# Another order of 68 units in a pipelined stack of convolutions, with VectorE's share of the evictions chosen unit by unit

## The reference, cut to what matters

```python
x = x + _L0_conv_ref(_gn(x), ...)   # windowed attention: qkv, scores + bias, softmax, weigh, projection
x = x + _L1_conv_ref(_gn(x), ...)   # one 3x3 convolution ("conv1")
x = x + _L2_conv_ref(_gn(x), ...)   # a grid of 4 columns x 4 rows of 3x3 convolution cells with relu
x = x + _L3_conv_ref(_gn(x), ...)   # a quantised 3x3 convolution, scaled by the maximum over all images
```

```python
for col in range(NUM_COLS):
    for row in range(NUM_ROWS):
        ...
        ins = [outs[row][0], outs[row + 1][1], outs[row - 1][-1]]   # inner rows; fewer at the edges
        outs[row] = _cell(W[col, row], b[col, row], ins)            # conv 3x3, bias, relu, split
return outs[-1][0]
```

## Time and profile before

| | |
|---|---|
| median of 3 runs | 3118.27 us (3115.51 to 3122.56) |
| profiled execution | 3120.86 us, span 3119.1 us |
| TensorE busy | 2786.1 us (89%) |
| VectorE busy | 2299.9 us (74%) |
| ScalarE busy | 2011.4 us (64%) |
| mean granted TensorE clock | 0.964 |

### The profile page before, as it was taken

One profiled execution on the slowest core, in us unless ns is written; L12 is line 12 of the kernel. 1 busy time (PEld: TensorE's weight loads), 2 busy tenths in 40 slices (PEclk: granted clock), 3 DMA queues, 4 the chain that ended last, 5 costly groups with the idle time before them and its releaser, 6 DMA issues.

```text
span 3119.1 us, 84833 instructions
## 1 busy us (share of the span) xinstructions
PE 2786.1 (89%) x39155; PEld 1185.7 (38%) x39155; DVE 2299.9 (74%) x2105; ACT 2011.4 (64%) x2318; POOL 23.5 (1%) x68
## 2 busy tenths in 40 slices
PE   4755899989998899989998999989998989889976
PEld 3742333333333333333433343333333333333333
DVE  8969985899688986889598987899599961240135
ACT  1107976766767676766776776767776775766524
POOL 0000000000000000000000000000000000000000
PEclk9877999999999999999999999999999999999998
DMA  1014656586667667675657766685657664775566
GB/s 63 11 21 63 84 79 91 72 111 89 85 84 95 94 84 99 80 105 79 84 84 92 102 89 90 86 113 74 94 74 99 90 88 64 94 107 73 79 89 181
DMA packets 37555, 268.00 MB, mean 86 GB/s; under 512 B 19280, under 2 KB 19920, under 8 KB 24784
## 3 DMA queue, kind: packets, MB, share of 16 engines
q1 hardware_dynamic: 37008, 261.77, 59.6%
q10 hardware_dynamic: 192, 0.80, 0.2%
HBM read 22.54 MB, written 12.04 MB: 11 GB/s over the span
## 4 chain that ended last, share of the span: by engine, by line
PE 70%; DVE 15%; ACT 10%; issue 3%; SPq 1%; DMA 1%; POOL 0%; ACTq 0%; POOLq 0%; DVEq 0%
PE conv_banks L856 43%; PE conv_banks L870 20%; ACT pair L706 5%; ACT half L706 4%; DVE pair L1058 2%; DVE half L1058 2%; PE side_banks L817 2%; PE stat_bank L827 1%; PE side_banks L783 1%; ACT scores L692 1%; PE conv_banks L954 1%; DMA half<-half 1%; DVE scores L1073 1%; DVE score_max L1081 1%; DVE scores L1071 1%
## 5 line engine op out<-in xcount | busy, mean ns | idle before, releaser
L706 ACT ACTIVATE pair<-conv_banks,b_cells 32x784 f32<-32x784 f32 x1316 | 1213.0, 922 | 586.9 <-PE conv_banks L870 520.0
L856 PE MATMUL conv_banks<-pair,w_cells 128*32 128x392 f32 x17664 | 1538.1, 497 | 25.2 <-issue 11.6
L870 PE MATMUL conv_banks<-half,w_cells 64*32 64x392 f32 x18432 | 880.2, 508 | 143.8 <-ACT pair L706 60.7
L856 PEld LDWEIGHTS conv_banks<-pair,w_cells 128*32 128x32 f32 x17664 | 559.6, 109 | 948.0 <-issue 904.3
L706 ACT ACTIVATE half<-conv_banks,b_cells 32x392 f32<-32x392 f32 (+1 forms) x780 | 520.4, 667 | 172.7 <-PE conv_banks L870 133.9
L870 PEld LDWEIGHTS conv_banks<-half,w_cells 64*32 64x32 f32 x18432 | 337.4, 107 | 666.6 <-issue 620.8
L1058 DVE TENSOR_SCALAR half<-conv_banks,b_cells 32x392 f32<-32x392 f32 (+1 forms) x180 | 114.4, 636 | 326.5 <-PE conv_banks L870 168.4
L1058 DVE TENSOR_SCALAR pair<-conv_banks,b_cells 32x784 f32<-32x784 f32 x220 | 227.5, 1034 | 109.3 <-PE conv_banks L870 99.1
L1071 DVE TENSOR_TENSOR scores<-qkv 128x1792 f32<-128x1792 f32 x98 | 197.8, 2019 | 71.8 <-ACT qkv L687 71.5
L692 ACT ACTIVATE scores<-scores 128x1792 f32<-128x1792 f32 x104 | 176.7, 1699 | 78.5 <-DVE scores L1155 46.1
L1097 DVE TENSOR_TENSOR scores<-scores,qkv 128x1792 f32<-128x1792 f32 x98 | 198.4, 2025 | 3.4
(11 more groups left out here) (107 smaller groups left out, 1042.3 us busy)
## 6 DMA issues: line engine op xcount, KB each, us to landing
pair<-pair SPq DMA_DIRECT2D x384, 391.9 KB, 8.6
half<-half SPq DMA_DIRECT2D x348, 192.4 KB, 5.6
x_block<-in_xa SPq DMA_DIRECT2D x8, 784.0 KB, 11.0
stream<-in_xs SPq DMA_DIRECT2D x8, 784.0 KB, 10.5
x_scratch<-stream SPq DMA_DIRECT2D x7, 784.0 KB, 6.9
pair<-x_scratch SPq DMA_DIRECT2D x7, 784.0 KB, 14.2
out_dram<-pair SPq DMA_DIRECT2D x4, 1120.0 KB, 5.3
half<-half SPq DMA_DIRECT2D x174, 7.1 KB, 4.7
```

The lines of the kernel that those rows point to most:

```text
L706: done = nc.scalar.activation(dst, src, ACT.Relu, bias=b_ap)
L856: done = nc.tensor.matmul(conv_ps[32 * q:32 * q + 32, n + b, 0:QN], w, P[row][:, QG * s + BG * (q // 2):QG * s + BG * (q // 2 + 1), BX * ( ...
L870: done = nc.tensor.matmul(conv_ps[32 * q:32 * q + 32, n + h, 0:QN], w_all[rows, at:at + 32], T[rows, QG * u + BG * (q // 2):QG * u + BG * ...
```

## The change

Three lists are replaced, and the code that reads them made finer.

- The order. Before, all units of a cell stood together. Now units of different cells alternate: column-0 units stand between units of other cells, and the two units of an output can stand apart. An asterisk marks the late units.
- VectorE's share. It is now a list of units, with the place in VectorE's own order: behind weigh 4, scores 6 and weigh 6, 17 units in a middle body (20 before). In body 6 it has 43 units (20 before), in body 7 10 (16 before), in body -1 one (none before). `move_stream` goes from behind weigh 9 to behind weigh 13.
- The side steps stand at other units, among them SyncE's "conv1", from 63 to 55 in the middle bodies.

```diff
-BODY = [((3, 0), 1), ((2, 2), 1), ((3, 1), 1), ((2, 3), 1), ((0, 0), 0), ((3, 2), 1), ((0, 1), 0), ((3, 3), 1),
-        ((0, 2), 0), ((1, 0), 0), ((0, 3), 0), ((1, 1), 0), ((1, 2), 0), ((2, 0), 0), ((1, 3), 0), ((2, 1), 0)]
+ORDER = """
+30D0* 30D1* 22D0* 22D1* 22U0* 22U1* 00R0 22R0* 22R1* 23U0* 23U1* 31D0* 31D1* 23R0* 00D0 23R1* 00D1
+32D0* 32D1* 00R1 01U0 01U1 01D0 01D1 33R0* 33R1* 01R0 10D0 10D1 02U0 01R1 02U1 02R0 10R0 02R1 02D0
+10R1 02D1 11D0 11D1 11U0 11U1 03U0 03U1 03R0 11R0 11R1 12U0 03R1 12U1 20D0 12D0 20D1 12D1 12R0 20R0
+12R1 13U0 13U1 20R1 13R0 13R1 21U0 21D0 21U1 21D1 21R0 21R1
+"""
...
-PE_MID = {2: [("qkv", 1, 0)], 7: [("proj", 0, 0), ("qkv", 2, 0)], 12: [("proj", 1, 0), ("qkv", 3, 0)],
-          27: [("proj", 2, 0), ("qkv", 4, 0)], 44: [("proj", 3, 0), ("qkv", 5, 0)],
-          49: [("proj", 4, 0), ("qkv", 6, 0)], 54: [("proj", 5, 0)], 59: [("proj", 6, 0)], 60: [("mean1", 0, 0)],
-          61: [("var1", 0, 0), ("mean0", 0, 1)], 62: [("var0", 0, 1)], 64: [("qkv", 0, 1)],
-          65: [("conv1", 0, 1)], 66: [("conv1", 1, 1)], 67: [("mean2", 0, 1), ("var2", 0, 1)]}
+PE_MID = {2: [("qkv", 1, 0)], 6: [("proj", 0, 0), ("qkv", 2, 0)], 13: [("proj", 1, 0)], 14: [("qkv", 3, 0)],
+          26: [("proj", 2, 0)], 29: [("qkv", 4, 0)], 42: [("proj", 3, 0)], 44: [("qkv", 5, 0)],
+          48: [("proj", 4, 0)], 49: [("qkv", 6, 0)], 57: [("proj", 5, 0)], 58: [("proj", 6, 0)],
+          59: [("mean1", 0, 0)], 60: [("var1", 0, 0), ("mean0", 0, 1)], 61: [("var0", 0, 1)],
+          63: [("qkv", 0, 1)], 64: [("conv1", 0, 1)], 65: [("conv1", 1, 1)], 66: [("mean2", 0, 1)],
+          67: [("var2", 0, 1)]}
...
-ACT_MID = {2: [("qkv", 1, 0), ("exp", 1, 0)], 5: [("exp", 2, 0)], 7: [("qkv", 2, 0), ("exp", 3, 0)],
-           9: [("exp", 4, 0)], 12: [("qkv", 3, 0), ("exp", 5, 0)], 19: [("exp", 6, 0)], 26: [("qkv", 4, 0)],
-           27: [("exp", 7, 0)], 38: [("exp", 8, 0)], 44: [("qkv", 5, 0), ("exp", 9, 0)], 47: [("exp", 10, 0)],
-           49: [("qkv", 6, 0), ("exp", 11, 0)], 51: [("exp", 12, 0)], 54: [("exp", 13, 0)], 64: [("qkv", 0, 1)],
-           65: [("exp", 0, 1)]}
+ACT_MID = {1: [("qkv", 1, 0)], 3: [("exp", 1, 0)], 5: [("exp", 2, 0)], 7: [("qkv", 2, 0)], 8: [("exp", 3, 0)],
+           10: [("exp", 4, 0)], 15: [("qkv", 3, 0)], 17: [("exp", 5, 0)], 24: [("exp", 6, 0)],
+           38: [("qkv", 4, 0)], 39: [("exp", 7, 0)], 41: [("exp", 8, 0)], 44: [("qkv", 5, 0), ("exp", 9, 0)],
+           46: [("exp", 10, 0)], 48: [("qkv", 6, 0)], 50: [("exp", 11, 0)], 54: [("exp", 12, 0)],
+           55: [("exp", 13, 0)], 63: [("qkv", 0, 1)], 64: [("exp", 0, 1)]}
...
-SP_MID = {35: [("x3", -1)], 48: [("xa", 2)], 63: [("conv1", 1)], 66: [("xb", 2)], 67: [("input", 1)]}
-SP_BEFORE = {35: [("x3", -1)], 62: [("conv1", 1)], 67: [("input", 1)]}
+SP_MID = {40: [("x3", -1)], 51: [("xa", 2)], 55: [("conv1", 1)], 67: [("xb", 2), ("input", 1)]}
+SP_BEFORE = {40: [("x3", -1)], 55: [("conv1", 1)], 67: [("input", 1)]}
...
+VEC_FIRST = {("s", 2): "00D0"}
+VEC_MID = {("w", 4): "23R0 00D0 23R1",
+           ("s", 6): "32D0 32D1 00R1 01U0 01U1 01D0",
+           ("w", 6): "02U0 01R1 02U1 02R0 10R0 02R1 02D0 10R1"}
+FINISH_AT = ("w", 6)
+MOVE_AT_FIRST, MOVE_AT = ("s", 13), ("w", 13)
+VEC_LATE = """30D0 22U0 22U1 23U1 31D0 31D1 23R0 00D0 23R1 32D0 32D1 00R1 01U0 01U1 01D0 01D1 10D0 10D1 02U0 01R1
+02U1 02R0 10R0 02R1 02D0 10R1 02D1 11D0 11D1 11U0 11U1 03U0 03U1 12U0 12D1 12R0 20R0 13U1 13R0 13R1
+21U0 21D1"""
+VEC_LAST = """22D0 22U1 22R0 22R1 23U1 31D1 23R0 23R1 32D0 32D1"""
...
-                for dst, src, b_ap in unit_operands(k, cell, o, u, range(2 if cell in shared_in(m) else NQ)):
+                for dst, src, b_ap in unit_operands(k, cell, o, u, range(2 if (cell, o, u) in shared_in(m) else NQ)):
...
+            def other_work(m, at):
+
+                early = isinstance(m, int) and m < 0
+                empty(m, units((VEC_FIRST if early else VEC_MID).get(at, "")))
+                if at == FINISH_AT and not early:
+                    finish(m, m)
+                if at == (MOVE_AT_FIRST if early else MOVE_AT):
+                    move_stream(m + 1)
```

More of the change, by code:

```diff
@@ L105, in strips_of, with unit, units, starts @@
     return (u, u + 2) if has_single(col, row) else (2 * u, 2 * u + 1)
-BODY = [((3, 0), 1), ((2, 2), 1), ((3, 1), 1), ((2, 3), 1), ((0, 0), 0), ((3, 2), 1), ((0, 1), 0), ((3, 3), 1),
-        ((0, 2), 0), ((1, 0), 0), ((0, 3), 0), ((1, 1), 0), ((1, 2), 0), ((2, 0), 0), ((1, 3), 0), ((2, 1), 0)]
[L111 to L119, removed]
+ORDER = """
[4 more added lines that the diff above has]
+"""
+def unit(text):
+    return (int(text[0]), int(text[1])), "RUD".index(text[2]), int(text[3])
+def units(text):
+    return [unit(t) for t in text.split()]
+UNITS = units(ORDER)
+UNITS_F = [unit(t) for t in ORDER.split() if t[4:] != "*"]
+UNITS_L = [unit(t) for t in ORDER.split() if t[4:] == "*"]
 NF, NB, NL = len(UNITS_F), len(UNITS), len(UNITS_L)
 NS = NF + (B - 1) * NB + NL
-def body_of(m):
-    return (EARLY_BODY if m < 0 else LATE_BODY if m == B - 1 else BODY) if isinstance(m, int) else BODY
 def units_in(m):
-    return units_of(body_of(m))
+    return (UNITS_F if m < 0 else UNITS_L if m == B - 1 else UNITS) if isinstance(m, int) else UNITS
+def starts(m, k):
+    done = units_in(m)
+    return done[k][0] not in [cell for cell, _, _ in done[:k]]
 def unit_base(m):
@@ L153, in count_halos @@
             wrote(m, "input", INPUT)
-        for (cell, late) in body_of(m):
-            need[m, cell] = [(key, n[key]) for key in in_places(*cell)]
-            for o in cell_outs(*cell) if cell != LAST else []:
+        for k, (cell, o, u) in enumerate(units_in(m)):
+            if starts(m, k):
+                need[m, cell] = [(key, n[key]) for key in in_places(*cell)]
+            if u == 1 and cell != LAST:
                 wrote(m, (cell, o), out_place(*cell, o))
-        if m == -1:
-            n_first = dict(n)
     return need
@@ L226, in n_shared @@
 def n_shared(m, end):
-    return sum(cell in shared_in(m) for cell, _, _ in units_in(m)[:end])
+    return sum(done in shared_in(m) for done in units_in(m)[:end])
 def vec_value(m, k):
-    ahead, per = n_shared(-1, NF), sum(cell in SHARED_MID for cell, _, _ in UNITS)
+    ahead, per = n_shared(-1, NF), len(SHARED_MID)
     if not isinstance(m, int):
@@ L880, in body @@
                         side_step(m + d, kind, j)
-                    if cell == (0, 0) and cell != seen:
+                    if cell == (0, 0) and starts(m, k):
                         wait_halos(pe, m, "input")
-                    conv_unit(m, k, cell, o, u, cell != seen).then_inc(conv_done, 1)
-                    seen = cell
+                    conv_unit(m, k, cell, o, u, starts(m, k)).then_inc(conv_done, 1)
             def first_sums(kind, k, done_sem):
@@ L1049, in normalise_stream, with empty @@
                     done.then_inc(c_ready, 1)
[L1051 to L1055, removed]
+            def empty(m, mine):
+                for cell, o, u in mine:
+                    k = units_in(m).index((cell, o, u))
                     dve.wait_ge(conv_done, unit_base(m) + k + 1)
@@ L1287, in move_stream, with late_body @@
                 done.then_inc(moved, 1)
-            def body(m):
[L1290 to L1301, removed]
+            def other_work(m, at):
[5 more added lines that the diff above has]
+                    move_stream(m + 1)
+            def late_body(m):
+                mine, end = shared_in(m), units_in(m).index((LAST, RIGHT, 1))
+                before = [u for u in mine if m == B - 1 or units_in(m).index(u) < end]
+                if m < B - 1:
+                    add_conv1(m + 1)
+                empty(m, before)
+                finish(m, m)
+                empty(m, mine[len(before):])
+                if m < B - 1:
+                    move_stream(m + 1)
+            def body(m):
                 i = m + 2
```

77 lines of the change are left out of this document (35 added, 42 removed).

## The result

The changed kernel takes 3133.11 us (median of 7 runs, 3125.78 to 3141.60); the kernel before takes 3118.27 (7 runs beside it, 3112.79 to 3122.56). The ratio is 1.0049, with a 95% interval of 1.0035 to 1.0064: 0.5% slower. The forecast was 3031 us in a range of 3002 to 3077, with a chance of 0.92 for faster. The profiled execution took 3125.78 us, with a span of 3124.0. Every median in this document is over executions that agree within 0.6%; one execution of experiment 1 took 9098 us and is in none of them.

What follows compares the result with a forecast made beforehand. TensorE was taken as the bound, with some 18 us idle per like body. Gains of 43 (five like bodies), 18, 13, 8 and 5 sum to 87 us: 3120.9 to 3033.9, or 3031 as median; range 3002 to 3077.

Steps and rivals of the forecast that it cites:

- a ring of waits between VectorE and ScalarE: Rival: late VectorE holds TensorE, then ScalarE's evictions and copies, so VectorE gets later; about 3129 us, chance 0.05.
- The half on the evictions: Like bodies: TensorE's waits for ScalarE's (27.5 us) and VectorE's (22.4 us) evictions over four bodies can be won by order.
- the last line of the walk: Like bodies: TensorE's waits under "issue" are removed by no order and stay at 1.6 us a body.
- so this costs nothing: SyncE's conv1 step from unit 63 to 55: four sends held behind it are first read 40 us later, so no cost.
- The eviction waits and the 4.26 us at 02U0: 02U0 to 11D0: 1.9 us of waits, none above 0.6; the 4.26 us wait and its slow clock go.
- The walk of a like body: 68 units walked in the new order: 12.0 us idle, body 336 us, 8.6 less than 344.6.
- the waits at the meeting points and the turns: TensorE's waits in four groups of units of a like body: about 1.0, 3.6, 1.9 and 2.7 us.
- VectorE at the last projection: Last projection, at 267 us of a like body: VectorE's wait falls from 8.18 us to at most 2.
- No copy or exponential was to come late: ScalarE's 34 copies and exponentials each end before VectorE asks; closest is chunk 5's copy, 196.1 against 197; no cost.
- Body 7: m = 7: 32D0's 6.22 us halo wait goes, the 11.66 us wait before 33R0 stays; 8 us less.
- Body -1: m = -1 (283.8 us): interleaving of cell (0, 3) and conv1 gives about 9 back, 00D0's wait costs 4; 5 us less.
- Bodies 5 and 6: m = 5 from 354.9 to 337 us, 18 less, with earlier halos; m = 6 from 323.7 to 310, 13 less.

Runs made afterwards that it cites:

- experiment 1: Changed kernel with SyncE's conv1 step back at its old places (before unit 63 in the middle bodies): 3111.7 us, ratio 0.998 to the kernel before.
- Experiment 2: Kernel before with only SyncE's conv1 step moved early, from before unit 63 to before unit 56: 3160.9 us, ratio 1.0126 to the kernel before.
- Experiment 5: Changed kernel with SyncE's conv1 step before unit 61 (43 in body -1): 3078.7 us, ratio 0.9862 to the kernel before.
- experiment 3: Changed kernel with each pair send from body 1 on moving half of its rows, same order, waits and DMAs: 3009.5 us, ratio 0.964 to the kernel before.

## Why the prediction was wrong

The direction was wrong, and so was the mechanism that decides it: none of the rivals named TensorE's own instructions. The rival that ended slower was a ring of waits between VectorE and ScalarE; TensorE's waits for their evictions fell instead of growing. The half on the evictions was right, and its gain is there: from span to span, waits for blocks cost 78.2 - 11.8 = 66.4 us more and busy time 14.6 more (2786.1 to 2800.7), and the span grew by 4.9, so all the rest gained 76.1 us.

**The failed step** is the last line of the walk, "Waits under "issue" in the list, which no order removes: 1.6 us a body". I took the item for a property of the program. It depends on what the DMA engines do at the time. It was measured at 12.6 us a body, and it brings half clock with it: TensorE's busy time is 330.8 us in the four bodies where 323.8 was forecast. So: 336 forecast, + 11.0 for issue, + 7.0 for the slow clock, - 3.4 for the other waits, which were 7.0 and not 10.4, is 350.6, against 350.4 measured in these four bodies.

**The step that led to it** is "so this costs nothing" for SyncE's conv1 step. I priced the sends behind the step by their readers, and for the readers it was right. What was left out is that held sends are released together. Experiment 2 prices it: 38 us in the old order. Experiment 5 gives 54 back in the new order against the changed kernel (58 by the ratios). The step at 63 avoids the burst too, but gives only 21 back, since it pays for the input's halos.

**Why the new order suffers more.** It asks for instructions faster. From 1366 to 1396.5 TensorE executes 462 + 451 instructions in 30.5 us, so a block of 254 lasts 8.5 us; the old order at its corresponding place, by the trace of before from 1360 to 1396, executes 456 + 440 in 36.0 us at a DMA share of 0.72, so a block lasts 10.2. The removed eviction waits (4.26 us at 02U0) may have given the fetch time to catch up. The rate alone costs nothing: experiment 3 runs the same instructions of this stretch in 27.6 us, with no such wait where the traffic is halved.

How much time a block has can be read from two traces of one program. I counted the matmuls and weight loads that TensorE had started when each block's transfer began. The block that began at 1397.14 came after 32,458 of them, and that is where TensorE stood; in experiment 3 the same block began after 32,203, 255 earlier. For all 25 waits for blocks of the changed kernel from body 1 on, TensorE stood still 165 to 291 instructions, 248 as a median, past the count at which the transfer of that block began in experiment 3. So with light traffic the fetch begins about one block ahead of the need: 8.5 us of cover at the new order's rate, and 10.2 at the old one's. That is why the same delay can cost the new order more. It is argued from these counts and windows; I made no run that slows the instructions and leaves the traffic, and the traffic differs too between the two windows (1.00 and 0.72).

**Point by point, the rest of the walk:**
- The eviction waits and the 4.26 us at 02U0 went, and the 0.54 clock of the earlier trace rows with it. Right.
- The walk of a like body: with the sends halved it is 330.1 us with 323.6 busy, so 6.5 idle. I had 336 with 323.8 busy and 12.0 idle. The busy time was right, and the idle terms were nearly twice too large: the waits at the meeting points and the turns, 9.2 us in the walk, came to 4.6, and the 1.6 of issue to none. The walk also has the two pair-only units at 4.02 us each where their row gives 4.10; that is too little to matter.
- VectorE at the last projection was to wait at most 2 us instead of the 8.18 of the earlier trace rows. It waits 1.30, so the cover was spent as forecast:

```profile
1505.83 0.45 DVE L1129 SCALAR_TENSOR_TENSOR stream<-stat_bank,b_proj_sb,stream 128x224 f32<-128x224 f32 x1 [1.30 <-PE stat_bank L849]
```

- No copy or exponential was to come late. In the changed kernel some did: behind the stop at 1396.5, VectorE waits 2.42 us for an exponential (1420.39) and 5.18 for a copy (1432.77), and over four bodies 8.5 us for exponentials. In experiment 3 neither is there: its one wait of this kind in a body, 7.8 us at scores 0, is shorter than the 11.15 of the kernel before. So the walk of ScalarE was right, and TensorE's stops broke it; TensorE lost little by that, since its own waits for VectorE stayed small.
- Body 7: 8 us forecast, 8.8 measured, and only the wait before 33R0 stays, as forecast:

```profile
3045.38 1.19 PE L868 MATMUL conv_banks<-pair,w_cells 128*32 128x392 f32 x4 [11.65 <-issue]
```

- Body -1: 5 forecast, 6.3 measured. Bodies 5 and 6: 18 and 13 forecast, 5.0 and 7.5 measured. These too have the waits for blocks (four in body 5, together 13.5 us, and two of 1.9 in body 6); with halved sends they take 328.3 and 304.6 us, where 337 and 310 were forecast.
- Together: 87 us forecast. With halved sends the order gives 73.4 against the old order, and 3009.5 us would lie inside the range. With all the bytes at better times it gives 3041.8. The range went by costs on the engines and in the readers of halos alone, and had no term for a cost of the traffic itself.

**What stays open.** Why the block that began at 1397.14 had to wait as long as it did. TensorE had reached the count at which experiment 3 fetches it at 1385.1, 12 us earlier. The Trainium skill, "DMA: Bandwidth & Descriptors", section "Queues, rings and completion order", says that a DMA engine takes packets from its rows in turn. By that a block would be held back by a packet or so (an estimate from the rule). A data packet lasts 0.921 x 16 x 11 us / 97 = 1.7 us on average from 1386 to 1397, so 12 us are several of them. This speaks against the rule as an account of the delay, but the trace does not show when a block is asked for, so it does not refute it. Spacings above 13.5 us between blocks exist in the kernel before as well (25 from 300 us on, against 21 in the changed one), so a long spacing alone does not make a wait.

## What to carry to other kernels

Idle time that is removed from the bound engine may have been what let something else keep up: look at the DMA share in windows of 20 to 30 us, not over a body, and at the instruction queue among the DMA queues, before an "issue" wait is called a constant. A run with the same DMAs and fewer bytes tells within one trace whether the traffic is the cause. A queue's step that waits for data turns every send behind it into a burst when it is released. Place it by that burst, and spread sends whose readers are far off; here three edits to the time of sends, without a byte less, turned 0.5% slower into 2.6% faster.

## What the hardware showed unexpectedly

- TensorE ran out of instructions in the middle of a unit, up to 5.2 us at a time in the changed kernel, while its 16 KB blocks shared the DMA engines with halo sends at a share of 0.93 as a median over the 25 us before, and 1.00 in the two stretches shown.
- With light traffic a block's transfer began some 248 instructions (165 to 291) ahead of where TensorE ran out with full traffic, so the cover is about one block, 8.5 us at 30 instructions per us.
- TensorE resumed 0.9 to 2.0 us after the end of the block, and the clock was 0.70 and 0.77 in the stretches of 11.5 and 7.4 us around two of these waits. The matmuls after the first took 188 ns each instead of 88, at a granted clock of 0.50, the lower of the two levels (1.2 of 2.4 GHz).
- Half of the pair bytes, with the same number of DMAs and packets, order and waits, took 3133.1 - 3009.5 = 123.6 us off the new order (some 128 by the ratios, as the two times were measured beside different runs of the kernel before) and 40.2 us off the old one.
